# Transposing token blocks by DMA through DRAM instead of on TensorE, in a scan layer with a quantized feed-forward layer

## What is computed

```
lam = sigmoid(u @ Wl.T + bl);  Bu = u @ Wb.T
h_t = lam_t * h_(t-1) + Bu_t                  # along the tokens
x1  = layernorm(u + (H @ Wc.T + u * Dp))
y   = (silu(x1 @ wg.T) * (x1 @ wu.T)) @ wd.T  # int32 weights / 127, hidden size 3072
out = layernorm(x1 + y)
```

## Time and profile before

| | |
|---|---|
| median of 3 runs | 1819.9 us (1819.48 to 1822.28) |
| the profiled execution | 1823.16 us |
| its span on the slowest core (core 7) | 1820.5 us |
| spans of the eight cores | 1808.6 to 1820.5 us |
| TensorE busy | 1449.1 us, 80% of the span |
| VectorE, ScalarE, GpSimd busy | 424.1, 326.9, 74.8 us |
| from 55 to 531.9 us | the scan part |
| from 606 to 694 us | the first norm |
| from 697 us | the feed-forward part |

### The profile page before, as it was taken

One profiled execution on the slowest core, in us unless ns is written; L12 is line 12 of the kernel. 1 busy time (PEld: TensorE's weight loads), 2 busy tenths in 40 slices (PEclk: granted clock), 3 DMA queues, 4 the chain that ended last, 5 costly groups with the idle time before them and its releaser, 6 DMA issues.

```text
span 1820.5 us, 18692 instructions; the slowest of 8 cores (1808.6 to 1820.5 us)
## 1 busy us (share of the span) xinstructions
PE 1449.1 (80%) x6832; PEld 711.3 (39%) x6832; DVE 424.1 (23%) x712; ACT 326.9 (18%) x507; POOL 74.8 (4%) x141
## 2 busy tenths in 40 slices
PE   2476776556656568999987999997999997999993
PEld 1233443333322354444434444443444443444441
DVE  2322230330225562121003212004121004212003
ACT  2011121211233452111002111002111002111001
POOL 0000000000000000000110000110000110000110
PEclk9977776677769768999997999997999997999996
DMA  2735556435220002222222222222222222222121
GB/s 70 150 91 140 124 119 127 107 86 131 64 64 1 1 1 80 77 76 76 72 62 94 80 76 76 71 68 90 79 76 75 72 73 86 77 76 76 52 70 52
DMA packets 84008, 142.77 MB, mean 78 GB/s; under 512 B 32208, under 2 KB 33232, under 8 KB 83920
## 3 DMA queue, kind: packets, MB, share of 16 engines
q1 hardware_dynamic: 35152, 70.27, 13.2%
q0 software_dynamic: 17472, 52.44, 12.1%
q10 hardware_dynamic: 31296, 18.88, 3.6%
HBM read 133.17 MB, written 27.26 MB: 88 GB/s over the span
## 4 chain that ended last, share of the span: by engine, by line
PE 68%; DVE 10%; DMA 8%; ACT 7%; issue 5%; DVEq 0%; ACTq 0%; SPq 0%; POOLq 0%; POOL 0%
PE ps L596 25%; PE pt L596 12%; PE ps L437 10%; PE ps L634 7%; PE pt L634 7%; DMA wbufd<-wdT_s 4%; ACT stg L280 3%; DMA wdT_s<-stgw 2%; PE ps L275 2%; DVE stat L222 2%; DVE u_hiF L413 1%; PE pt L398 1%; DVE u_loF L416 1%; DVE res L647 1%; ACT t2b L515 1%
## 5 line engine op out<-in xcount | busy, mean ns | idle before, releaser
L596 PE MATMUL ps<-x1hi,wbufg 128*128 128x512 bf16 x768 | 295.4, 385 | 5.0 <-DMA wbufg<-wgT_s 5.0
L596 PE MATMUL ps<-x1lo,wbufg 128*128 128x512 bf16 x768 | 295.1, 384 | 0.0
L596 PE MATMUL pt<-x1hi,wbufu 128*128 128x512 bf16 x512 | 194.0, 379 | 0.0
L596 PE MATMUL pt<-x1lo,wbufu 128*128 128x512 bf16 x512 | 194.0, 379 | 0.0
L634 PE MATMUL ps<-hh_hi,wbufd 128*128 128x512 bf16 x384 | 145.2, 378 | 8.1 <-DMA wbufd<-wdT_s 6.5
L634 PE MATMUL pt<-hh_hi,wbufd 128*128 128x512 bf16 x384 | 145.5, 379 | 0.0
L634 PE MATMUL pt<-hh_lo,wbufd 128*128 128x512 bf16 x384 | 145.5, 379 | 0.0
L634 PE MATMUL ps<-hh_lo,wbufd 128*128 128x512 bf16 x384 | 145.4, 379 | 0.0
L612 ACT ACTIVATE hh_hi<-hhf 128x512 bf16<-128x512 f32 x96 | 60.4, 630 | 345.0 <-DVE hhf L606 345.0
L217 PE MATMUL pt<-id,res 128*128 128x128 f32 x256 | 57.3, 387 | 79.0 <-DVE mv L226 34.5
L275 PE MATMUL ps<-idbf,cvgu 128*128 128x128 bf16 x384 | 46.6, 297 | 87.0 <-ACT stg L280 64.1
(11 more groups left out here) (79 smaller groups left out, 1325.7 us busy)
## 6 DMA issues: line engine op xcount, KB each, us to landing
wbufg<-wgT_s SPq DMA_DIRECT2D x96, 256.0 KB, 2.6
wbufu<-wuT_s SPq DMA_DIRECT2D x96, 256.0 KB, 2.6
wbufd<-wdT_s POOLq DMA_DIRECT2D x96, 256.0 KB, 2.9
utok<-u_pre SPq DMA_DIRECT2D x16, 512.0 KB, 4.2
utok<-u_main SPq DMA_DIRECT2D x16, 512.0 KB, 4.1
out<-x1tok POOLq DMA_DIRECT2D x16, 512.0 KB, 2.9
cvwd<-wd POOLq DMA_DIRECT2D x8, 768.0 KB, 15.8
cvgu<-wg POOLq DMA_DIRECT2D x6, 1024.0 KB, 12.6
```

The source lines that it names most:

```text
L596: lambda e: e.matmul(o, l, r, start=st_, stop=sp_)))(
```

## The change

In the scan part a group of u is no longer transposed on TensorE. VectorE splits it as rows, from SBUF, into `uhb` and `ulb`; ScalarE's queue writes both to a DRAM array `u_s`; and when all four groups of a block are written, SP issues 16 DMAs with transpose, each from 512 tokens by 128 features of `u_s` to 128 partitions by 512 tokens of `u_hiF` or `u_loF`. In the norm part the same is done with `x1tok` through `x1_s`: ScalarE makes the hi part, VectorE the rest, ScalarE's queue writes them, SP issues 16 transposing DMAs a block into `x1hi` and `x1lo`. The names of the tokens change with it, one for a block of 512 tokens. `sc.fence` gives the present counts of the named semaphores, and the step waits for them.

```diff
                         utok[sl][:, :], rows),
                         writes=[("utok", sl)], sem=f"qu{sl}", n=16)
-                    for dc in range(DC):
-                        sc.step("tensor", (lambda o, s: (lambda e: e.transpose(o, s, id32[:, :])))(
-                            pt[g % 2][:, dc * P:(dc + 1) * P],
-                            utok[sl][:, dc * P:(dc + 1) * P]),
...
+                    sc.step("vector", (lambda o, s: (lambda e: e.tensor_copy(out=o, in_=s)))(
+                        uhb[sl][:, :], utok[sl][:, :]),
+                        reads=[("utok", sl)], writes=[("uhb", sl)])
+                    sc.step("vector", (lambda o, s, h: (lambda e: e.tensor_tensor(
+                        out=o, in0=s, in1=h, op=OP.subtract)))(
+                        ulb[sl][:, :], utok[sl][:, :], uhb[sl][:, :]),
+                        reads=[("utok", sl), ("uhb", sl)], writes=[("ulb", sl)])
+                    srow = st * ST + g * P
+                    sc.step("scalar", (lambda d, s: (lambda e: e.dma_start(out=d, in_=s)))(
+                        u_s[0, srow:srow + P, :], uhb[sl][:, :]),
+                        reads=[("uhb", sl)], writes=[("us0", st, g)], sem=f"qus{sl}", n=16)
+                    sc.step("scalar", (lambda d, s: (lambda e: e.dma_start(out=d, in_=s)))(
+                        u_s[1, srow:srow + P, :], ulb[sl][:, :]),
+                        reads=[("ulb", sl)], writes=[("us1", st, g)], sem=f"qul{sl}", n=16)
+                lane = f"qt{st}"
+                wrdeps = sc.fence(["qus0", "qus1", "qul0", "qul1"])
+                for dc in range(DC):
+                    for (hl, arena) in ((0, u_hiF), (1, u_loF)):
+                        sc.step("sync", (lambda d, s: (lambda e: e.dma_start(
+                            out=d, in_=s, transpose=True)))(
+                            arena[:, dc * TL + s4 * ST: dc * TL + (s4 + 1) * ST],
+                            u_s[hl, st * ST:(st + 1) * ST, dc * P:(dc + 1) * P]),
+                            extra_deps=wrdeps, writes=[("uarena", s4)], sem=lane, n=16)
...
                 ln_group(lambda dc, gg=gg: res1[:, dc * TL + gg * P: dc * TL + (gg + 1) * P],
                          g, lambda dc, s4=s4: [("res1", dc, s4)])
+                sc.step("scalar", (lambda o, sp: (lambda e: e.copy(out=o, in_=sp)))(
+                    x1hb[sl][:, :], x1tok[g][:, :]),
+                    reads=[("x1tokbuf", g)], writes=[("x1hb", sl)])
+                sc.step("vector", (lambda o, sp, h: (lambda e: e.tensor_tensor(
+                    out=o, in0=sp, in1=h, op=OP.subtract)))(
+                    x1lb[sl][:, :], x1tok[g][:, :], x1hb[sl][:, :]),
+                    reads=[("x1tokbuf", g), ("x1hb", sl)], writes=[("x1lb", sl)])
...
+            wrdeps = sc.fence(["qxs0", "qxs1", "qxl0", "qxl1"])
+            lane = f"qxt{s4}"
             for dc in range(DC):
-                for g in range(4):
-                    sc.step("tensor", (lambda o, sp: (lambda e: e.transpose(o, sp, id32[:, :])))(
-                        bank(dc)[:, g * P:(g + 1) * P],
...
+                for (hl, arena) in ((0, x1hi), (1, x1lo)):
+                    sc.step("sync", (lambda d, sp: (lambda e: e.dma_start(
+                        out=d, in_=sp, transpose=True)))(
+                        arena[:, dc * TL + s4 * ST: dc * TL + (s4 + 1) * ST],
+                        x1_s[hl, s4 * ST:(s4 + 1) * ST, dc * P:(dc + 1) * P]),
+                        extra_deps=wrdeps, writes=[("x1arena", s4)], sem=lane, n=16)
```

More of the change, by code:

```diff
@@ L148, in build_nc @@
     out_h = nc.dram_tensor("out", [TL, D], F32, kind="ExternalOutput").ap()
+    u_s = nc.dram_tensor("u_s", [2, T, D], BF16).ap()
+    x1_s = nc.dram_tensor("x1_s", [2, TL, D], BF16).ap()
     wgT_s = nc.dram_tensor("wgT_s", [HC, P, D], BF16).ap()
@@ L363, in build_nc @@
             utok = [AE(nc.sbuf_tensor(f"utok{k}", [P, D], F32)) for k in range(2)]
+            uhb = [AE(nc.sbuf_tensor(f"uhb{k}", [P, D], BF16)) for k in range(2)]
+            ulb = [AE(nc.sbuf_tensor(f"ulb{k}", [P, D], BF16)) for k in range(2)]
             lam_sb = [AE(nc.sbuf_tensor(f"lam{k}", [P, ST], F32)) for k in range(NCC)]
@@ L388, in emit_A0 @@
                 s4 = st % NST
-                par = st % 2
                 src = u_pre if pre else u_main
@@ L396, in emit_A0 @@
                         writes=[("utok", sl)], sem=f"qu{sl}", n=16)
-                    for dc in range(DC):
-                        sc.step("tensor", (lambda o, s: (lambda e: e.transpose(o, s, id32[:, :])))(
-                            pt[g % 2][:, dc * P:(dc + 1) * P],
-                            utok[sl][:, dc * P:(dc + 1) * P]),
-                            reads=[("utok", sl), "id32"],
-                            writes=[("pb", 4 + 2 * (g % 2) + dc // 4)],
-                            lazy=(dc < DC - 1))
@@ L432, in emit_mm @@
                         wlo = wlbT_lo[:, (j * DC + dc) * P:(j * DC + dc) * P + P]
-                        for (lhsT, rhs, rt) in [(whi, rhs_hi, ("uhit", s4)),
-                                                (whi, rhs_lo, ("ulot", s4)),
-                                                (wlo, rhs_hi, ("uhit", s4))]:
+                        for (lhsT, rhs, rt) in [(whi, rhs_hi, ("uarena", s4)),
+                                                (whi, rhs_lo, ("uarena", s4)),
+                                                (wlo, rhs_hi, ("uarena", s4))]:
                             sc.step("tensor", (lambda o, l, r, st_, sp_: (
@@ L513, in build_nc @@
                             out=o, in0=a, in1=b2, op=OP.add)))(usum[dc % 2][:, :], uh, ul),
-                            reads=[("uhit", tt), ("ulot", tt)], writes=[("usum", dc % 2)])
+                            reads=[("uarena", tt), ("uarena", tt)], writes=[("usum", dc % 2)])
                         sc.step("scalar", (lambda o, s, scl: (lambda e: e.activation(
@@ L532, in build_nc @@
         x1tok = lnb["x1tok"]
+        x1hb = [E(nc.sbuf_tensor(f"x1hb{k}", [P, D], BF16)) for k in range(2)]
+        x1lb = [E(nc.sbuf_tensor(f"x1lb{k}", [P, D], BF16)) for k in range(2)]
         x1hi = E(nc.sbuf_tensor("x1hi", [P, DC * TL], BF16))
@@ L538, in build_nc @@
                 gg = s4 * 4 + g
+                sl = g % 2
                 ln_group(lambda dc, gg=gg: res1[:, dc * TL + gg * P: dc * TL + (gg + 1) * P],
                          g, lambda dc, s4=s4: [("res1", dc, s4)])
-            for dc in range(DC):
-                for g in range(4):
-                    sc.step("tensor", (lambda o, sp: (lambda e: e.transpose(o, sp, id32[:, :])))(
-                        bank(dc)[:, g * P:(g + 1) * P],
[L545 to L555, removed]
@@ new lines, in build_nc @@
+                sc.step("scalar", (lambda d, sp: (lambda e: e.dma_start(out=d, in_=sp)))(
+                    x1_s[0, gg * P:(gg + 1) * P, :], x1hb[sl][:, :]),
+                    reads=[("x1hb", sl)], sem=f"qxs{sl}", n=16)
+                sc.step("scalar", (lambda d, sp: (lambda e: e.dma_start(out=d, in_=sp)))(
+                    x1_s[1, gg * P:(gg + 1) * P, :], x1lb[sl][:, :]),
+                    reads=[("x1lb", sl)], sem=f"qxl{sl}", n=16)
+            wrdeps = sc.fence(["qxs0", "qxs1", "qxl0", "qxl1"])
@@ L590, in build_nc @@
                             (x1hi[:, dc * TL + m * ST: dc * TL + (m + 1) * ST],
-                             ("x1hi", dc, m)),
+                             ("x1arena", m)),
                             (x1lo[:, dc * TL + m * ST: dc * TL + (m + 1) * ST],
-                             ("x1lo", dc, m)),
+                             ("x1arena", m)),
                         ]:
@@ L645, in build_nc @@
                     out=o, in0=a, in1=b2, op=OP.add)))(x1s[sl][:, :], uh, ul),
-                    reads=[("x1hi", dc, m), ("x1lo", dc, m)], writes=[("x1s", sl)])
+                    reads=[("x1arena", m), ("x1arena", m)], writes=[("x1s", sl)])
                 sc.step("vector", (lambda o, s, a: (lambda e: e.scalar_tensor_tensor(
```

## The result

The changed kernel takes 2173.6 us against 1821.9 us of the kernel before: a ratio of 1.193, 95% interval 1.1905 to 1.195. The forecast was 2201 us. Some executions of an eight-core program run disturbed, with a lower clock on one die; the ratios here leave them out, and where a kernel's time is given alone it is of an undisturbed run.

A forecast was written before the change was run, and what follows sets the result against it. The prediction took transposing DMAs in series on SP, each waiting for the last to land, as the bound. Scan part +224 and norm part +157 made +381 us, 2201 us on the median; range 1960 to 2750, held at 0.81.

The forecast's parts named there:

- The bound: Scan and norm parts: each transposing DMA is issued only when the one before has landed, 16 a stage in series.
- The size of t: Norm part: time from issue to landing of one transposing DMA, taken as 3.3 us, with ends 2.2 and 7.7.
- plain copy: Rival, both parts: t is a plain DMA's, 2.2 to 2.9 us; 1992 us at 2.6, 1926 at 2.2; chance 0.20.
- Small pieces on the written side: Rival, both parts: 32 byte pieces set t, up to 7.7 us, 3111 us; chances 0.20 (t 4.2 to 6), 0.12 (above).
- the band of the forecast: Whole kernel: t from 2.9 to 4.2 us, that is 2115 to 2379 us, chance 0.43.
- t' in the scan part: Scan part: issue to landing of one transposing DMA, a fifth above t for transfers running beside it, 4.0 us.
- The first stage: Scan part: first transposing DMA at about 82.5, first matmuls mm(0) at 146.5 instead of 80.6 us.
- The round: Scan part: SP's loads, waits for split and writes, and DMAs set the period, 19.7 + 15 x 4.0 = 79.7 us.
- what would show it: Signs: issues 4.0 and 3.3 us apart, matmul bursts 80 us apart, TensorE idle before them, norm part 244 us.
- The norm part: First layer norm's window: 64 DMAs run on end and hide the norm, 33 + 64 x 3.3 = 244 us, +157.
- The sum: Whole kernel: scan part +224 and norm part +157 make +381 us; in general 121 t' + 64 t - 314.5.
- The rival "overlap": Both parts: the 16 DMAs don't wait, issued 0.45 us apart; scan +12 - 57, norm +43, about 1818 us; chance 0.03.

The follow-up runs named there:

- e1_overlap: The changed kernel with a block's 16 transposing DMAs no longer waiting for each other, readers still waiting for all 16: ratio 1.050, 1909 us.
- e5_plain_copy: The changed kernel with every transposing DMA replaced by a plain one of the same bytes and the same waits: 2110 us.
- e10_halves: Against the kernel with only the norm part changed, each transposing DMA cut into two of 256 tokens, still in series: 2074.9 us.
- e6_prep_late: The changed kernel with all weight preparation moved behind the eight blocks of the scan part: 2226.9 us.
- e11_prefetch: e8_sp_writes with four utok buffers and the next block's loads issued ahead of the 16 transposing DMAs: ratio 0.986 of the kernel before, 1795 us.
- e8_sp_writes: Changed kernel without waits between DMAs, norm part as before, block 0 transposed on TensorE, DRAM writes on SP's queue: ratio 1.0032 of the kernel before, 1827 us.
- e3_norm_only: The kernel before with the change in the norm part alone, the scan part as before: ratio 1.067, 1941.6 us.

## Why the prediction was right

*The bound.* Both halves of the change were forecast as a series of 64 or 128 DMAs, each waiting for the last writer of a token that all share. SP's rows and e1_overlap show it: without the wait 264 of 352 us go.

*The size of t, taken from dp_sb as 3.3 us (ends 2.2 and 7.7).* It was 2.87 in the norm part, and its undisturbed median 2.6 to 2.7, the value of the rival "plain copy". e5_plain_copy and e10_halves show why: two microseconds of latency, 0.2 to 0.4 us for the turning. Small pieces on the written side, for which 7.7 us stood, cost nothing that can be seen. The wide upper part of the range wasn't needed. So the time lies in the band of the forecast (t 2.9 to 4.2), and t itself at the upper end of the rival's band, 2.2 to 2.9.

*t' in the scan part, taken as 4.0.* It was 4.08 in blocks 1 to 7, but not as a fifth more than 3.3: it was half as much again as 2.69 (e6_prep_late). Two errors of opposite sign met; the scan part's sum was right for a partly wrong reason, and that is luck. With the t that was measured, 2.87, and only a fifth on 2.69, t' would be 3.2, the sum +261 and the time 2081 us, below the forecast's own band. That the DMAs stand in series was foreseen; that other transfers lengthen them by half was not.

*The first stage.* mm(0) was forecast at 146.5 and began at 134.9. Its DMAs ran nearly undisturbed, 16 in 43.7 us, which is 2.7 us each, 20 less than forecast; but the first went out at 91.2, not 82.5, because two of the writes to DRAM, forecast at 2.6 us each, took 16.6 and 9.9 us. They ran beside the first weight loads, with the DMA engines busy throughout (a share of 0.99 to 1.06 from 60 to 91 us).

*The round.* 81.0 us against 79.7; 18.5 us ahead of the DMAs against 19.2. TensorE waits 346 us for the DMAs of u, as "what would show it" said. VectorE's copy from SBUF took 0.69 us for 128x1024, half the 1.38 that I took, its subtraction 1.23. The groups by line show the copy:

```profile
L402 DVE CAST uhb<-utok 128x1024 bf16<-128x1024 f32 x32 | 22.1, 692 | 462.0 <-DMA utok<-u_main 257.6 <-DMA utok<-u_pre 203.0 <-DMA u_s<-uhb 1.4
```

*The norm part.* +128.6 against +157: the first DMA went out at 32.4 us (forecast 33), a group took 6.75 us (7.2) and hid behind SP; the miss is all in t, 64 x 0.43.

*The sum.* +349.5 between the spans against +381, of which 27 us are t in the norm part. One reading is slightly off: the prediction ends the transposes of a period at 112.3 and names, where L299 stands at 112.51. By that row they cost 8.5 us a period and not 8.2, which changes nothing in the sum.

*The rival "overlap"* was priced at 1818 us and its kernel, e1_overlap, takes 1909. Its term for the norm part held (forecast +43, measured +49), its gain of 45 us in the scan part did not. It took 0.45 us for an issue on SP; a transposing DMA's is 1.11, and they go out 1.25 us apart, so 16 of them take 20 us and not 7. The step that failed there is that with t' out of the way TensorE's periods bound the scan part. Load latencies, VectorE, writes and 16 issues of 1.25 us still make a round on SP as long as the old period; it took a deeper prefetch (e11_prefetch) to get half of the gain.

## What to carry to other kernels

Count the DMAs that stand in series before asking how fast each is: the cost was number times latency, 192 x about 3.5 us, and neither halving a DMA's bytes (0.37 us) nor a plain copy (0.2 to 0.4 us) changed much. When a scheduler tracks a buffer by one token, look whether several writers of separate parts of it wait for each other; a wait by count on one semaphore does the same for the reader. Work moved from a compute engine to a DMA queue paid here only when that queue's own round, loads and issues included, was shorter than the compute engine's old period (a period of 53.0 us in e11_prefetch, 57.1 before).

## What the runs showed of the hardware

- A transposing DMA of 512x128 bf16 from DRAM landed in 2.6 to 2.7 us in the median, and without the wait they went out 1.25 us apart (e1_overlap); a plain DMA of the same size landed in 2.4. A transposing DMA's issue held SP for 1.11 us against 0.36, and, where several were in flight, now and then for up to 12.3 us (e8_sp_writes, DMA share 0.78) and 16.8 us (e11_prefetch, 0.97).
- Two transposing DMAs of 256x128 took 2 x 2.42 us in series (e10_halves), one of 512x128 took 2.79 (e3_norm_only).
- Beside the weight preparation's transfers a DMA of 128 KB took up to 16.7 us to land, and 4.08 us a step on average instead of 2.69; the median moved only from 2.6 to 2.7.
- VectorE's float32 to bf16 copy of 128x1024 from SBUF took 692 ns, as long as 128x512 from PSUM before; the subtraction gained little (1225 ns for 128x1024, against twice 692 before).
- DMA engines moved 208 GB/s at a share of 0.97 in e11_prefetch, with pieces of 256 bytes among them.
- TensorE's granted clock in the changed kernel's norm part was 0.51, nearly its lower level, with TensorE busy 29 of 219 us; before it was 0.68 with 49 of 91. The feed-forward part behind it had 0.95 and the same length, so the idle time left no trace there.
